# Gate and up of a feed-forward as a 2x2 block product with seven products, weights streamed

## The reference

```python
HID, INTER = 512, 1376
w = (qweight >> 4 * j) & 15                    # 8 numbers of each int32
W = (w - (zeros[g_idx] + 1)) * scales[g_idx]   # for gate, up and down

def ffn(x):                                    # Wg, Wu: 512 x 1376, Wd: 1376 x 512
    h = silu(x @ Wg) * (x @ Wu)
    return h @ Wd

def attn(x):
    q, k, v = split(x @ Wqkv + bqkv)           # 128 columns each
    p = softmax(q @ k.T / sqrt(128))
    return (p @ v) @ Wo + bo

x = x + 0.5 * ffn(layernorm(x))
x = x + attn(layernorm(x))
x = x + 0.5 * ffn(layernorm(x))
```

## Time and profile before

| | |
|---|---|
| time, median of 3 runs | 909.29 us (909.21 to 910.09) |
| span of the profiled execution | 905.7 us |
| TensorE busy | 879.3 us (97%), 4238 instructions |
| VectorE busy | 355.5 us (39%) |
| ScalarE busy | 232.6 us (26%) |
| GpSimd busy | 147.6 us (16%) |
| DMA | 62.77 MB, 69 GB/s on the mean |

### The profile page before, as it was taken

The page is one execution under the profiler, slowest core; times in us unless marked ns, Lnnn a source line. Parts: engine busy times, 40 slices in busy tenths (PEclk is TensorE's granted clock), DMA queues, the critical chain, the costliest instruction groups (busy, mean ns, idle before and its releaser), DMA issues.

```text
span 905.7 us, 10861 instructions
## 1 busy us (share of the span) xinstructions
PE 879.3 (97%) x4238; PEld 717.0 (79%) x4238; DVE 355.5 (39%) x647; ACT 232.6 (26%) x395; POOL 147.6 (16%) x128
## 2 busy tenths in 40 slices
PE   5999999999999999998998999999999999999998
PEld 4676778888888888886887888888888888888886
DVE  6877752212322232337777543223222322231112
ACT  1332331112111211113664654331111211121111
POOL 6434320000000002003064145540000000000000
PEclk9999999999999999999999999999999999999999
DMA  5556514000400041006042326311200120011001
...
DMA packets 47554, 62.77 MB, mean 69 GB/s; under 512 B 9996, under 2 KB 20924, under 8 KB 47516
## 3 DMA queue, kind: packets, MB, share of 16 engines
...
q10 hardware_dynamic: 1152, 1.36, 0.6%
...
## 4 chain that ended last, share of the span: by engine, by line
PE 89%; DVE 4%; DMA 3%; SPq 2%; ACT 1%; issue 1%; POOL 0%; DVEq 0%; POOLq 0%; ACTq 0%
PE ps L516 84%; PE ps L528 2%; DVE xn L1023 1%; PE ps L741 1%; SPq L376 1%; DMA shift<-in_shifts 1%; DMA wf<-in_L_attn_Wo 1%; DMA saved<-wf 1%; DVE wf L1058 1%; DVE wi L1050 1%; DMA qs<-in_L_ffn_gate_qweight 1%; PE ps L578 1%; PE ps L523 1%; DVE xT_odd L1030 0%; DVE stats L1007 0%
## 5 line engine op out<-in xcount | busy, mean ns | idle before, releaser
L516 PE MATMUL ps<-xT,weights 128*128 128x512 f32 (+1 forms) x2112 | 498.2, 391 | 0.8 <-POOL weights L1254 0.7
L516 PEld LDWEIGHTS ps<-xT,weights 128*128 128x128 f32 (+1 forms) x2112 | 389.5, 185 | 91.7 <-issue 2.3
L516 PE MATMUL ps<-weights,hT 128*128 128x512 f32 (+1 forms) x1056 | 256.2, 391 | 0.0
L1082 DVE TENSOR_TENSOR hs<-hs,ps 128x512 f32<-128x512 f32 (+1 forms) x88 | 60.4, 686 | 438.4 <-PE ps L516 438.4
L516 PEld LDWEIGHTS ps<-weights,hT 128*128 128x128 f32 (+1 forms) x1056 | 196.5, 188 | 40.8
L860 ACT ACTIVATE hs<-ps 128x512 f32<-128x512 f32 (+1 forms) x88 | 52.5, 597 | 285.1 <-PE ps L516 285.1
L868 ACT ACTIVATE hT<-hs 128x512 fp32r<-128x512 f32 (+1 forms) x88 | 55.6, 632 | 236.4 <-DVE hs L1082 236.4
L1104 DVE TENSOR_TENSOR hT<-hs,hT 128x512 fp32r<-128x512 f32 (+1 forms) x88 | 61.2, 695 | 32.8 <-ACT hT L868 32.8
L1250 POOL TENSOR_TENSOR rstd<-rstd,mhalf 128x4 f32<-128x4 f32 x12 | 12.7, 1058 | 363.0 <-DVE rstd L1017 363.0
L1254 POOL TENSOR_TENSOR weights<-wf,weights 128x512 fp32r<-128x512 f32 (+2 forms) x33 | 43.3, 1311 | 62.2 <-ACT weights L838 62.1
L1254 POOL TENSOR_TENSOR weights<-wback,weights 128x512 fp32r<-128x512 f32 (+2 forms) x27 | 34.6, 1309 | 32.0 <-ACT weights L845 32.0
...
## 6 DMA issues: line engine op xcount, KB each, us to landing
...
xn<-stream SPq DMA_DIRECT2D x6, 1024.0 KB, 6.0
...
xn<-in_L_attn_x SPq DMA_DIRECT2D x3, 1024.0 KB, 6.0
```

Source lines behind the costliest of these rows:

```text
L516: mm = pe.matmul(bank_ap, lhs(a), rhs(b), start=first and n == 0, stop=last and n == 2)
L1082: dve.tensor_tensor(out=hs[0:w, i % 2, :], in0=hs[0:w, i % 2, :], in1=ps[0:w, 2 * pair + 1, :], op=ALU.mult).then_inc(s_h, 1)
```

## The change

The feed-forward runs in pairs of 1024 tokens (`pair` and `bottom`). The input is a block matrix of 2 x 2: token halves by halves of the inner dimension (A11, A12 for the top tokens, A21, A22 for the bottom ones); the weights are another, B: halves of the inner dimension by gate and up. With S1 = A21 + A22, S2 = S1 - A11, S3 = A11 - A21, S4 = A12 - S2 and T1 = B12 - B11, T3 = B22 - B12, T2 = B22 - T1, T4 = B21 - T2, the seven products are P1 = A11 B11, P2 = A12 B21, P5 = S1 T1, P6 = S2 T2, P7 = S3 T3, P3 = S4 B22 and P4 = A22 T4, each over half the inner dimension (2 tiles x 3 passes = 6 matmuls). Gate of the top is P1 + P2; the other three are sums of P1 and P6 with P7, P5, P3 or P4. Some of these sums are matmuls that go on in a bank, the others are VectorE's (`middle`, `up_bottom`, `gate_bottom`, `up_top`). The S sums are made once for each pair by VectorE, hi on ScalarE, lo on VectorE (S3, S4) and GpSimd (S1, S2); the T sums by GpSimd while the weights are made.

The weights of gate and up are no longer all in SBUF. A block (seven factors, hi and lo, 1.83 MB) is made in one of two slots of `ring`, stored whole (`save_block`), and read again for each tile of the three later pairs (`load_block`), in two parts; part 0 waits until product 2 of the tile that had the slot is done, part 1 for its product 3. Down's weights stay. Down of the top tokens goes along with the tiles; the bottom tokens' result is kept in `h2` for all 11 tiles and its down blocks follow in `bottom`, where the next tokens are turned too. There are three slots of hT instead of two. In the first pair zeros and scales go through one bank, one after the other, each copied out by ScalarE (`zeros_of`, `scales_of`, `zeros_out`, `scales_out`); VectorE works from these copies. ScalarE normalises groups 0, 1 and 3, GpSimd 2, 4, 5, 9, 10 and 11, VectorE 6, 7 and 8. Groups 4 and 5 are turned in `bottom(1)`. Before the second feed-forward A11 and A12 are turned in attention, A21 and A22 around its last product, and S2, S3 and S4 are made from hi and lo parts, two VectorE operations for each half. No hardware loop is left.

```diff
+A11, A12, S1, S2, S3, A22, S4 = range(7)
+A21 = 7
+P1, P2, P5, P6, P7, P4, P3 = range(7)
+PAIRS = 4
...
+        blk = place("blk", [P, 7, 2, 2, ROWS], F32R)
+        ring = place("ring", [P, 2, 7, 2, 2, P], F32R)
+        h2 = place("h2", [P, NT, ROWS], F32)
...
+            def save_block(i):
+                sp.wait_ge(s_wlo, 4 * (i + 1))
+                for part in range(2):
+                    chip, kept = block_sides(i, part)
+                    sp.dma_start(kept, chip).then_inc(d_save[i % 2], 16)
+            def load_block(n):
+                i = n % NT
+                sp.wait_ge(d_save[i % 2], saves_of(i))
+                if n - 2 < NT:
+                    sp.wait_ge(d_save[n % 2], saves_of(n - 2))
+                for part in range(2):
+                    if n == 2 * NT + 2 and part == 0:
+                        sp.wait_ge(s_P7, n - 1)
+                    elif n not in (2 * NT, 2 * NT + 1):
+                        sp.wait_ge((s_P2, s_P3)[part], n - 1)
+                    chip, kept = block_sides(n, part)
+                    sp.dma_start(chip, kept).then_inc(d_ring[n % 2][part], 16)
...
-            def gate_up(i, m, pair, kts=range(KT), by_tile=False):
...
-                for k in kts:
...
-                    mm = product(ps[0:w, 2 * pair + m, :], lambda h: weights[:, i, h, m, k * P:k * P + w],
-                                 lambda h: xT[:, h, k, :],
-                                 k == 0, k == KT - 1)
...
+            def product(q, which, bank, slot, i, onto=False):
+                w = width(i)
+                for kt in range(2):
+                    for n, (a, b) in enumerate(PASSES):
+                        mm = pe.matmul(ps[0:w, bank, :], ring[:, slot, which, a, kt, 0:w], blk[:, which, b, kt, :],
+                                       start=not onto and kt == 0 and n == 0, stop=kt == 1 and n == 2, skip_group_check=onto)
+                return mm
...
+            def dequant_step(i, place):
+                if i == 1:
+                    if place == 0:
+                        scales_of(unit_of(2, 0))
+                        return
+                    place -= 1
+                m = place // 2 + (2 if i == NT - 1 else 0)
+                if m > 2:
+                    return
+                u = unit_of(m, i + 1 if m < 2 else i)
+                if place % 2:
+                    scales_of(u)
+                else:
+                    zeros_of(u)
...
+            def product_1(q, i):
+                n = NT * q + i
+                if q == 0:
+                    pe.wait_ge(s_wlo, 4 * i + 1)
+                else:
+                    pe.wait_ge(d_ring[n % 2][0], 16 * ring_loads(n))
+                if i == 0:
+                    pe.wait_ge(s_xlo, split(q, A11, 1))
+                    if q == 2:
+                        pe.wait_ge(s_exp, 2 * QT)
+                else:
+                    pe.wait_ge(s_g1, n)
+                product(q, P1, product_bank(q, 0), n % 2, i).then_inc(s_P1, 1)
...
+                    pe.wait_ge(s_slo12, summed_lo(q, S2, 1))
...
+                pe.wait_ge(s_u2, n + 1)
+                product(q, P7, product_bank(q, 1), n % 2, i, True).then_inc(s_P7, 1)
...
+                pe.wait_ge(s_u3, n + 1)
+                product(q, P4, product_bank(q, 1), n % 2, i, True).then_inc(s_P4, 1)
...
+                pe.wait_ge(s_c22, n + 1)
+                product(q, P3, product_bank(q, 2), n % 2, i, True).then_inc(s_P3, 1)
...
+            def pair(q, first=0):
+                for i in range(first, NT):
+                    product_1(q, i)
+                    product_6(q, i)
+                    product_5(q, i)
+                    product_2(q, i)
+                    product_7(q, i)
+                    if i:
+                        top_down(q, i - 1)
+                    product_4(q, i)
+                    product_3(q, i)
...
+            def bottom(q):
+                down(q, 1, 0)
+                down(q, 1, 1)
+                top_down(q, NT - 1)
+                first, second = {0: (4, 7), 1: (2, 4), 2: (2, 5), 3: (NT, NT)}[q]
+                for i in range(2, NT):
+                    down(q, 1, i)
...
+            pe.wait_ge(s_ln[1], RT)
+            turn_block(0, A21, 0)
+            turn_block(0, A21, 1)
+            pe.wait_ge(s_x21, 1)
+            turn_block(0, A22, 0)
+            pe.wait_ge(s_x21, 2)
+            turn_block(0, A22, 1)
+            product_1(0, 0)
+            product_2(0, 0)
+            product_6(0, 0)
+            zeros_of(unit_of(0, 1))
+            product_5(0, 0)
+            scales_of(unit_of(0, 1))
+            product_7(0, 0)
+            zeros_of(unit_of(1, 1))
+            product_4(0, 0)
+            scales_of(unit_of(1, 1))
+            product_3(0, 0)
+            first_down_tables()
+            zeros_of(unit_of(2, 0))
+            for i in range(1, NT):
...
+                            pe.wait_ge(s_ln[9], RT)
+                            turn_block(2, A21, 0)
+                            turn_block(2, A21, 1)
+                            turn_block(2, A22, 0)
                     pv(b, g)
                 if b:
-                    gate_up(0, 1, pair_of(BACK, 0))
+                    pe.wait_ge(s_x21, 5)
...
+            zeros_out(0)
+            scales_out(0)
+            x_hi(0, A11, 0)
+            x_hi(0, A11, 1)
+            zeros_out(1)
+            scales_out(1)
+            x_hi(0, A12, 0)
+            x_hi(0, A12, 1)
+            ln_apply(1)
+            gate_hi(0)
+            x21(0, 0)
+            x21(0, 1)
+            first_out(0)
+            x_hi(0, A22, 0)
+            x_hi(0, A22, 1)
+            differences_hi(0)
+            up_hi(0)
+            for kt in range(2):
+                sum_hi(0, S1, kt)
+            for kt in range(2):
+                sum_hi(0, S2, kt)
+            silu_top(0)
+            zeros_out(unit_of(0, 1))
...
+            def middle(n):
+                w = width(n % NT)
+                dve.wait_ge(s_p1, n + 1)
+                dve.wait_ge(s_P6, n + 1)
+                plus(u2[0:w, n % 2, :], ps[0:w, product_bank(n // NT, 1), :], p1s[0:w, n % 2, :]).then_inc(s_u2, 1)
+            def up_bottom(n):
+                w, q = width(n % NT), n // NT
+                if n >= 2:
+                    dve.wait_ge(s_h2, n - 1)
+                dve.wait_ge(s_P7, n + 1)
+                plus(u3[0:w, n % 2, :], ps[0:w, product_bank(q, 1), :], p1s[0:w, n % 2, :]).then_inc(s_u3, 1)
+                dve.wait_ge(s_u3, n + 1)
+                plus(u3[0:w, n % 2, :], ps[0:w, product_bank(q, 2), :], u3[0:w, n % 2, :]).then_inc(s_c22, 1)
+            def gate_bottom(n):
+                i = n % NT
+                w = width(i)
+                dve.wait_ge(s_P4, n + 1)
+                plus(h2[0:w, i, :], ps[0:w, product_bank(n // NT, 1), :], p1s[0:w, n % 2, :]).then_inc(s_c21, 1)
+            def up_top(n):
+                w = width(n % NT)
+                dve.wait_ge(s_P3, n + 1)
+                plus(u2[0:w, n % 2, :], ps[0:w, product_bank(n // NT, 2), :], u2[0:w, n % 2, :]).then_inc(s_u1, 1)
+                dve.wait_ge(s_u1, n + 1)
+                dve.wait_ge(s_g1, n + 1)
+                dve.tensor_tensor(out=u2[0:w, n % 2, :], in0=u2[0:w, n % 2, :], in1=g1[0:w, n % 2, :], op=ALU.mult)\
+                    .then_inc(s_h1, 1)
+            def top_lo(q, i):
+                e, n, w = use(q, 0, i), NT * q + i, width(i)
+                dve.wait_ge(s_hhi, e + 1)
+                minus(hT[0:w, e % 3, 1, :], u2[0:w, n % 2, :], f32(hT[0:w, e % 3, 0, :])).then_inc(s_hlo, 1)
...
+            def gate_lo(i):
+                pool.wait_ge(s_whi, 4 * i + 1)
+                part = slice(P1, P2 + 1)
+                minus(parts_of(i, part, 1), base_blocks(i)[:, 0:2, :, :], f32(parts_of(i, part, 0))).then_inc(s_wlo, 1)
+            def differences(i):
+                w, base = width(i), base_blocks(i)
+                if i:
+                    pool.wait_ge(s_wlo, 4 * i)
+                pool.wait_ge(s_wf, unit_of(1, i) + 1)
+                minus(t13[:, :, :, 0:w], base[:, 2:4, :, :], base[:, 0:4:2, :, :]).then_inc(s_t, 1)
+                pool.wait_ge(s_t, 3 * i + 1)
+                minus(t24[:, 0, :, 0:w], base[:, 3, :, :], t13[:, 0, :, 0:w]).then_inc(s_t, 1)
+                pool.wait_ge(s_t, 3 * i + 2)
+                minus(t24[:, 1, :, 0:w], base[:, 1, :, :], t24[:, 0, :, 0:w]).then_inc(s_t, 1)
+            def differences_lo(i):
+                pool.wait_ge(s_whi, 4 * i + 3)
+                part = slice(P6, P3, 2)
+                minus(parts_of(i, part, 1), t24[:, :, :, 0:width(i)], f32(parts_of(i, part, 0))).then_inc(s_wlo, 1)
+                part = slice(P5, P4, 2)
+                minus(parts_of(i, part, 1), t13[:, :, :, 0:width(i)], f32(parts_of(i, part, 0))).then_inc(s_wlo, 1)
+            def up_lo(i):
+                pool.wait_ge(s_whi, 4 * i + 4)
+                part = slice(P3, P3 + 1)
```

(20 more changed lines are left out.)

1585 lines of the change are left out of this document (1015 added, 570 removed).

## The result

The changed kernel takes 922.06 us (median of 4 runs, 919.35 to 923.79), the kernel before 909.25 us (906.56 to 910.09) beside it. The ratio is 1.0135, with a 95% interval of 1.011 to 1.0161: slower by 1.1 to 1.6%, where 888 us was forecast. The profiled execution took 922.75 us and spans 920.9 us, 15.2 us more than the kernel before and 36.4 us more than the forecast's 884.5.

The account below looks back on a forecast made before the run. TensorE, busy 879.3 of 905.7 us, was taken as the bound. 905.7 - 59.8 + 17.3 + 12.4 - 6.1 + 12.1 + 2.9 (clock) = 884.5 us of span, forecast 888 us; range 875 to 906.

Parts of the forecast that it names:

- Products: Gate and up: 42 matmuls a step instead of 48, 264 fewer at 0.2267 us each, -59.8 us.
- The ring and changes of bank: Plain pair: streamed blocks arrive within the 12.24 us step and bank changes with satisfied waits are free; cost nothing.
- The steps that dequantise: First pair, ten steps of 15.0 us instead of 12.24, with 66 table groups for 33: +12.4 us, bounds +5 to +22.
- the bounds on a group: Half a table group of scales or zeros costs 0.35 us, between 0.28 (half) and 0.56 (whole).
- The second rival: VectorE, slowed beside GpSimd, bounds the steps making weights: 17.7 us a step, +27, 915 us; chance 0.13.
- the rule: Trainium skill: two-input VectorE operations from SBUF contend with GpSimd reading SBUF; the loser is blocked for its whole length.
- The start: Before regular steps: 48.1 us of other things, 19.2 more than before; +17.3 us, bounds +8 to +30, plus 1.6 for clock.
- The first bottom stage: In `bottom`, hi and lo halves and VectorE's turned tiles and sums lie beside the down blocks; costed at nothing.
- Attention: The 4.5 us wait at 424 and the half clock after it, 1.6 us, go: -6.1 us.
- Transition: Into the second feed-forward: normalisation of t=9 +3.7, sums +8.4; +12.1 us, bounds +6 to +18, plus 1.3 for clock.
- The first rival: Hand-overs cost more than worked out: steps of 16.0, start 5 us later, +15, 903 us; chance 0.17.
- The slower side: The outcome that the changed kernel is slower than before: chance 0.12, against faster 0.86 and same 0.02.

Follow-up runs that it names:

- the run with small loads: Changed kernel with streamed weight-block loads moving one of 128 partitions, except the first two of the third pair: span 922.8 us against 920.9.
- the fillers: Changed kernel plus filler matmuls in TensorE's idle stretches of the start, 28 ahead of P6 and 10 ahead of P7: 916.18 us, ratio 1.0077.
- the new order: Changed kernel with the first pair's S2 and S1 low halves moved from GpSimd to VectorE, S4's sum and ScalarE's S4/S3 highs earlier: 916.63 us, ratio 1.0083.

## Why the prediction was wrong, point by point

- **Products, -59.8 us: right.** 264 matmuls went at the price of 0.2267 us, and a plain step is 12.24 us. The ring and changes of bank cost nothing, as put, and the product waits next to nothing (3.2 us for `u` in four waits of the whole execution); the run with small loads shows it for the stream.
- **The steps that dequantise, +12.4 us: 23.1, above the upper bound of 22.** The step that failed is "half a group is 4 x 0.053 = 0.21 of streaming and the rest fixed: 0.35". It took the eight of before as one behind another, so that half of them would save 0.21 us. They overlapped (0.41 us for eight, each four busy for 0.4 of it); a group of four takes 0.22 and the break 0.34, and nothing is saved. Six times 0.21 too little is 1.25 us a step, the difference between 15.0 and 16.25; that it is all of it is in part luck, since the wait for ScalarE's copy was 0.66 instead of 0.45, and the 0.2 put for a late `up_top` did not show at TensorE. The earlier trace rows held the group of eight and nothing that separated the two parts, though the view of the same trace by form, shown above, does; the bounds on a group said so (0.28 to 0.56), and the measured value was their upper end.
- **The second rival: right in kind, wrong in size.** VectorE is slowed beside GpSimd, by 0.55 and 0.90 us on the mean in two groups with both inputs in SBUF and by 0.35 in the unpack, but not in all, and would set about 15.5 us a step, not 17.7. It is not what made the kernel slower, since TensorE's 16.0 lies above it. The row that I held against the rule, a mean of 0.76 us, is of the right form but was taken where GpSimd was 45% busy, and here it is 71%: the same low half takes 1683 ns. And the 675 ns of the same rows belong to an instruction that reads its zeros from PSUM. The change gives it both inputs in SBUF, and 1234 ns. "By the row it is not" rested on a row under a lighter load, and the 0.68 in the sum of VectorE's work on one of another form.
- **The start, +17.3 and 1.6 of clock: 30.3, at the upper end of the bounds (+8 to +30), 11.4 off.** The order of waits was as forecast (P6 for GpSimd, P7 for S3's low half, a table for ScalarE). Mis-sized was the way to product 1: "copies zeros and scales and turned tiles for units 0 and 1 (to 21.9)" lasted to 26.5, where ScalarE stood idle between the copies for TensorE's table groups, and the 16 turns of A21 and A22 took 3.77 us. P1 came at 32.8 instead of 27.0, P6 at 46.1 instead of 39.9. And the clock: six of the seven products of the first step took 2.55 to 2.93 us instead of 1.6, nearly 7 us in all where 1.6 was put. From P1 to the third down block the fillers gave 3.6 us back and the new order 6.5.
- **The first bottom stage, at nothing: 8.8.** The sentence that failed is "I cost both at nothing". The cover was counted against VectorE's and ScalarE's work on halves and sums. Two things at that place were not costed at all: the statistics of the third row block, for whose load VectorE stood 2.33 us, and its normalisation, new on GpSimd: 8.26 us, a power behind it, and VectorE waiting for that power with the next low half in its queue. The edit that moves both gave 8.4 us back.
- **Attention, -6.1: -7.5, right.** The wait and the half clock behind it went.
- **Transition, +12.1 and 1.3: 16.0, inside the bounds (+6 to +18).** Both waits were named; the normalisation's was 3.63 (3.7 forecast), P6 came 22.4 us behind the request instead of 15.8 (544.4 + 3.7 - 532.3), behind turns and heads at half clock; products 5, 7 and 4 followed it closer than worked out, so that 2.6 us remain.
- **The cases.** The first rival (hand-overs dearer, step of 16.0, start 5 us later, 903 us) is nearest: its step of 16.0 nearly held, though by the price of the groups and not by hand-overs, and the rest of the start and a bottom stage priced at nothing made most of the other 19 us. The slower side was reached without its mechanism, by four terms all missed in one direction.
